# Last pass of a six-pass graph network on one core: rows closed in another order, four chunks' layers computed from split parts, steps spaced wider, adjacency splits queued 14 pieces ahead instead of 20

## The reference, cut to what matters

```python
# x: 4096 x 128, adj: 4096 x 4096, all float32
def gnn(x, adj, kernel, bias):                 # one product with adj, one layer
    return relu((adj @ x) @ kernel + bias)

def mlp(x, W1, b1, W2, b2, W3, b3):            # three 128 x 128 layers
    x = leaky_relu(x @ W1 + b1, 0.01)
    x = leaky_relu(x @ W2 + b2, 0.01)
    return leaky_relu(x @ W3 + b3, 0.01)

x = layernorm(x + gnn(x, adj, ...))
u = x
for _ in range(3):
    v = mlp(adj @ u, uv weights)
    u = mlp(adj @ v, vu weights)               # the third u is never used
x = layernorm(x + v)
```

## Time and profile before

| | us |
|---|---|
| median of 3 runs | 1168.94 |
| lowest and highest | 1168.66, 1168.98 |
| the profiled execution, its own time | 1168.49 |
| its span in the profile | 1166.7 |
| PE busy | 1153.5 (99% of the span) |
| DVE busy | 736.7 (63%) |
| ACT busy | 659.3 (57%) |

### The profile page before, as it was taken

The page is one execution under the profiler, slowest core; times in us unless marked ns, Lnnn a source line. Parts: engine busy times, 40 slices in busy tenths (PEclk is TensorE's granted clock), DMA queues, the critical chain, the costliest instruction groups (busy, mean ns, idle before and its releaser), DMA issues.

```text
span 1166.7 us, 13724 instructions
## 1 busy us (share of the span) xinstructions
PE 1153.5 (99%) x5242; PEld 954.0 (82%) x5242; DVE 736.7 (63%) x888; ACT 659.3 (57%) x811; POOL 4.9 (0%) x10
## 2 busy tenths in 40 slices
PE   7999999999999999999999999999999999999998
PEld 6888888888888888888888888888888888887876
DVE  7997676458555555555545746553566554678985
ACT  7765555346554555555444755553556544667874
POOL 0000000000000000000000000000000000000001
PEclk9999999999999999999999999999999999999999
DMA  9988786568356646555656636655575656579971
GB/s 383 405 301 322 251 270 198 200 216 288 120 205 217 210 157 213 199 195 181 205 188 220 238 124 211 205 179 198 192 242 165 212 186 230 166 292 356 312 281 36
DMA packets 72353, 261.60 MB, mean 224 GB/s; under 512 B 8032, under 2 KB 8800, under 8 KB 71264
## 3 DMA queue, kind: packets, MB, share of 16 engines
q1 hardware_dynamic: 72144, 260.61, 64.0%
q10 hardware_dynamic: 144, 0.13, 0.0%
HBM read 258.61 MB, written 2.10 MB: 223 GB/s over the span
## 4 chain that ended last, share of the span: by engine, by line
PE 94%; DMA 3%; DVE 1%; ACT 0%; SPq 0%; issue 0%; ACTq 0%
PE agg_ps L932 29%; PE agg_ps L925 28%; PE agg_ps L918 28%; PE pre_ps L829 4%; DMA adj_raw<-in_adj 3%; PE hid_ps L790 1%; PE hid_ps L792 1%; PE hid_ps L791 1%; DVE adj_lo L770 1%; PE hid_ps L851 1%; PE hid_ps L865 0%; ACT adj_hi L635 0%; DVE stats L648 0%; PE hid_ps L868 0%; SPq L496 0%
## 5 line engine op out<-in xcount | busy, mean ns | idle before, releaser
L770 DVE TENSOR_TENSOR adj_lo<-adj_raw,adj_hi 128x1024 fp32r<-128x1024 f32 x464 | 547.8, 1219 | 224.9 <-ACT adj_hi L635 219.6
L918 PE MATMUL agg_ps<-adj_hi,feat_hi 128*128 128x512 f32 x1484 | 586.4, 395 | 7.5 <-ACT adj_hi L635 7.5
L925 PE MATMUL agg_ps<-adj_hi,feat_lo 128*128 128x512 f32 x1484 | 579.3, 390 | 0.0
L635 ACT ACTIVATE adj_hi<-adj_raw 128x1024 fp32r<-128x1024 f32 x464 | 467.6, 1051 | 83.3 <-PE agg_ps L932 69.1
L932 PE MATMUL agg_ps<-adj_lo,feat_hi 128*128 128x512 f32 x1484 | 458.8, 390 | 0.2 <-DVE adj_lo L770 0.2
L918 PEld LDWEIGHTS agg_ps<-adj_hi,feat_hi 128*128 128x128 f32 x1484 | 279.6, 188 | 66.0 <-issue 9.4
L925 PEld LDWEIGHTS agg_ps<-adj_hi,feat_lo 128*128 128x128 f32 x1484 | 279.5, 188 | 59.1 <-issue 1.9
L932 PEld LDWEIGHTS agg_ps<-adj_lo,feat_hi 128*128 128x128 f32 x1484 | 278.9, 188 | 59.5 <-DVE adj_lo L770 1.1
L528 ACT ACTIVATE hid<-hid_ps,params 128x512 f32<-128x512 f32 (+2 forms) x82 | 55.1, 672 | 59.6 <-PE hid_ps L792 50.7
L600 ACT ACTIVATE in_hi<-part 128x512 fp32r<-128x512 f32 x24 | 15.2, 634 | 110.3 <-DVE part L759 110.3
L528 ACT ACTIVATE post<-pre 128x512 f32<-128x512 f32 x39 | 24.7, 632 | 88.0 <-DVE pre L737 88.0
(11 more groups left out here) (80 smaller groups left out, 389.8 us busy)
## 6 DMA issues: line engine op xcount, KB each, us to landing
adj_raw<-in_adj SPq DMA_DIRECT2D x472, 512.0 KB, 5.6
adj_raw<-in_adj SPq DMA_DIRECT2D x8, 1024.0 KB, 8.1
resid<-in_x SPq DMA_DIRECT2D x8, 256.0 KB, 8.1
out<-resid SPq DMA_DIRECT2D x7, 256.0 KB, 5.3
params<-in_weights SPq DMA_DIRECT2D x1, 386.0 KB, 5.1
b_row<-in_bias_rows SPq DMA_DIRECT2D x1, 128.0 KB, 5.7
out<-resid SPq DMA_DIRECT2D x2, 64.0 KB, 1.8
out<-resid ACTq DMA_DIRECT2D x1, 128.0 KB, 1.9
```

The lines of the kernel that those rows point to most:

```text
L635: act.activation(split_hi(b)[:, i * CHUNK:(i + pieces) * CHUNK], adj_raw[:, h % RAW, 0:pieces * CHUNK], ACT.Copy).then_inc(adj_hi_ready, 1)
L770: dve.tensor_tensor(split_lo(b)[:, slot], adj_raw[:, h % RAW, 0:pieces * CHUNK], split_hi(b)[:, slot].bitcast(F32), ALU.subtract).then_inc ...
L918: pe.matmul(group_bank(g), feat_hi[feats][:, tile(src, i)], split_hi(b)[:, piece(i)], start=start, stop=False)
L925: pe.matmul(group_bank(g), feat_lo[feats][:, tile(src, i)], split_hi(b)[:, piece(i)], start=False, stop=False)
```

## The change

The rows of the last pass are closed in the order 6, 1, 5, 4, 3, 2 (before: 6, 5, 4, 3, 1, 2). The first four chunks of the last pass (rows 0, 7, 6 and 1) are computed in parts, with a table of their own, LAST_PARTS. The LATE3 table goes, and LATE2 and LATE get wider distances. LAST_LEAD goes from 20 to 14.

```diff
-LEAD, FIRST_LEAD, LAST_LEAD, FIRST_ROWS = 12, 4, 20, 3
+LEAD, FIRST_LEAD, LAST_LEAD, FIRST_ROWS = 12, 4, 14, 3
...
+    LAST_PARTS: dict(dve_sum=0, act_in=3, dve_in=4, pe_hid1=10, act_hid1=11, dve_hid=13, pe_hid2=20, act_hid2=21,
+                     pe_out=25, dve_pre=25, act_post=28, dve_stats=29, act_std=32, dve_shift=33, act_norm=36),
     LAST: dict(dve_sum=0, act_in=0, pe_hid1=6, act_hid1=7, pe_hid2=10, act_hid2=11, pe_out=14, dve_pre=14,
                act_post=16, dve_stats=16, act_std=20, dve_shift=20, act_norm=24),
-    LATE3: dict(dve_sum=0, act_in=0, pe_hid1=6, act_hid1=7, pe_hid2=10, act_hid2=11, pe_out=14, dve_pre=14,
-                act_post=16, dve_stats=17, act_std=20, dve_shift=20, act_norm=24),
-    LATE2: dict(dve_sum=0, act_in=1, pe_hid1=4, act_hid1=5, pe_hid2=7, act_hid2=8, pe_out=9, dve_pre=10,
-                act_post=10, dve_stats=12, act_std=14, dve_shift=15, act_norm=16),
-    LATE: dict(dve_sum=0, act_in=1, pe_hid1=1, act_hid1=2, pe_hid2=3, act_hid2=5, pe_out=5, dve_pre=7, act_post=7,
-               dve_front=8, dve_total=8, dve_stats=9, act_std=12, dve_root=13, pool_norm=13),
+    LATE2: dict(dve_sum=0, act_in=0, pe_hid1=5, act_hid1=6, pe_hid2=9, act_hid2=10, pe_out=13, dve_pre=13,
+                act_post=14, dve_stats=15, act_std=18, dve_shift=18, act_norm=22),
+    LATE: dict(dve_sum=0, act_in=1, pe_hid1=3, act_hid1=4, pe_hid2=5, act_hid2=7, pe_out=7, dve_pre=9, act_post=9,
+               dve_front=10, dve_total=10, dve_stats=11, act_std=14, dve_root=15, pool_norm=15),
...
-LAST_ROWS = (6, 5, 4, 3, 1, 2)
+LAST_IN_PARTS = 4
+LAST_ROWS = (6, 1, 5, 4, 3, 2)
...
             return END2 if after < 0 else END if after == 0 else LATE if after == 1 else LATE2 if after == 2 \
-                else LATE3 if after == 3 else LAST
+                else LAST_PARTS if u < self.rows * (PASSES - 1) + LAST_IN_PARTS else LAST
...
-        return self.steps_of(u) in (IN_PARTS, TURN)
+        return self.steps_of(u) in (IN_PARTS, TURN, LAST_PARTS)
...
-                u = at(t, "dve_hid", HIDDEN)
+                u = at(t, "dve_hid", DEEP)
...
-                u = at(t, "dve_in", HIDDEN)
+                u = at(t, "dve_in", DEEP)
```

More of the change, by code:

```diff
@@ L40 @@
 HOLD = 3
-LEAD, FIRST_LEAD, LAST_LEAD, FIRST_ROWS = 12, 4, 20, 3
+LEAD, FIRST_LEAD, LAST_LEAD, FIRST_ROWS = 12, 4, 14, 3
 LOAD_GCN, LOAD_PARAMS = 24, 90
 W_SPLIT = 320
-IN_PARTS, TURN, LATE3, LATE2, LATE, END, END2 = "in_parts", "turn", "late3", "late2", "late", "end", "end2"
+IN_PARTS, TURN, LAST_PARTS, LATE2, LATE, END, END2 = "in_parts", "turn", "last_parts", "late2", "late", "end", "end2"
 STEPS = {
```

## The result

| | before | changed |
|---|---|---|
| median of 6 runs, us | 1168.72 | 1174.73 |
| lowest and highest | 1168.45, 1168.98 | 1174.15, 1174.85 |
| profiled execution | 1168.49 | 1174.76 |
| its span | 1166.7 | 1173.0 |

What follows compares the result with a forecast made beforehand. PE, busy 99% of the span, was taken to bound the kernel, with DVE near its limit. Waits of 7.8, less 0.3 waited before and 1.5 saved, gave +6.0: 1174.5 profiled, 1175.0 median, range 1172.5 to 1177 (62%).

Steps and rivals of the forecast that it cites:

- Part 1: PE's own work: eight float32 layers computed in parts save 0.185 us each, 1.5 us less.
- Part 2: Added work on DVE and ACT in the last pass makes PE wait at late steps, 7.8 us in all.
- first place: Second layer of row 6: DVE's `hid_lo` starts at 1103.0, so PE waits 1.6 us.
- all rounds: DVE's waits for ACT in the three stretches laid out: 1.8, 2.3 and 2.8 us.
- Second place: Second layer of row 5: ACT's hidden layer is late, PE waits 2.6 us, and 0.8 at the third layer.
- Third place: First layer of row 4: DVE's sum starts at 1140.4, so PE waits 1.8 us.
- The clock: Rival, 3%: waits of 2.6 us twice lower PE's granted clock, +3 us more, 1178.
- Part 3: What costs nothing: splits stay ahead of their use, wider tables fit; the lead alone is worth 0.3 us.
- The end: From the last row's cuts on, same operations in the same order: costed at nothing.
- DVE keeps up: Rival, 10%: DVE's 51.8 us of work fit PE's 53.3, PE keeps its 1.5 us gain: 1167.4.
- Half of it: Rival, 15%: only the first and third place are late, 3.5 us of waits, +1.7: 1170.6.
- Feed each other: Rival, 10%: late steps delay the next rows, another wait of 2 to 3 us at row 3 or final cuts: 1178.

Runs made afterwards that it cites:

- four_moved: Changed kernel with dve_hid 12 instead of 13, act_post 29 instead of 28, act_norm 39 instead of 36, lead 16 instead of 14, same work: 1167.23 us.
- five_placed: Changed kernel with a fifth chunk (row 5) in parts, five numbers of LAST_PARTS moved and lead 20: 1166.37 us.
- busy_pe: Changed kernel with nine added, never-read products on PE ahead of its wait for row 5's second layer: 1174.56 us.
- parts_only: Kernel before with rows 0, 7, 6 and 5 in parts by LAST_PARTS and row 4 by LAST; row order, LATE2, LATE and lead unchanged: 1171.85 us.
- lead20: Changed kernel with LAST_LEAD 20 again instead of 14: 1174.51 us.
- no_parts: Changed kernel with no chunk of the last pass in parts; row order, wider tables and lead of 14 kept: 1168.96 us.
- norm38: Changed kernel with act_norm of LAST_PARTS 38 instead of 36, so ACT's scaling stands two ticks later: 1170.48 us.
- norm34: Changed kernel with act_norm of LAST_PARTS 34 instead of 36, so ACT's scaling stands two ticks earlier: 1182.82 us.

## Why the prediction was right, and where not

The forecast was 1175.0, the measurement 1174.73. By its own steps, the excess at each place taken from distances between L933 rows, as above:

| step of the prediction | forecast | measured |
|---|---|---|
| second layer of row 6, waits for `hid_lo` | 1.6 | 1.7 |
| the small waits before row 5 | 0.4 + 0.2 | 0.3 + 0.2 |
| second layer of row 5, waits for ACT | 2.6 | 2.3 |
| slow clock behind it (a rival's, 3%) | 0 | 1.7 |
| third layer of row 5 | 0.8 | 0 |
| first layer of row 4, waits for `part` | 1.8 | 1.0 |
| first layer of row 3 | 0.4 | 0.6 |
| sum | 7.8 | 7.8 |
| waited before; layers in parts (both as in part 1) | -0.3 - 1.5 | -0.3 - 1.5 |

This makes +6.0, as forecast. The profiled execution became 6.27 us longer; what is more lies within the 0.37 by which it is behind already when row 0 closes. 0.33 of that are there at 300 us, where both kernels do the same, so it has nothing to do with the change.

The sum is right and its parts are not. PE's waits add up to 6.1 us and not 7.8 (the prediction expected 7 to 8 in the profile; the view of waits, which counts from modelled ends, has 4.6), and 1.7 us of slow matmuls stand in for the rest. That the total came out even so is in part luck, and in part the reason given under the clock.

**Part 1** is right: four_moved, where PE waits for almost nothing, is 1.4 us faster than before, and five_placed, with two layers more in parts, 2.4; 1.5 and 1.85 were to come from the layers and 0.3 from the wait that there was before, less the 0.5 left over in four_moved. That gives 1.3 and 2.15.

**Part 2, first place.** `hid_lo` was to start at 1103.0 and started at 1103.33; row 0 closed 0.37 us later than in the trace of before (ACT's copy starts at 1062.05 instead of 1061.68), and taken from there the step is exact. The step on which it rested, DVE's four waits for ACT, 1.8 in all, measured 0.52 + 0.34 + 0.24 + 0.29 = 1.4 in brackets. Each also costs the 0.09 us by which DVE's operations otherwise overlap (a split is 1.22 long and the next starts after 1.13), which makes 1.75. Over all rounds I had laid out 1.8 + 2.3 + 2.8 = 6.9. The view has 6.8, but that holds a wait of 1.24 that ended at 1079.99, ahead of the rounds; the other eleven are 5.6, or 6.6 with 0.09 for each. Where they come from I had laid out wrongly in part: ACT was to stand at the root each time, and of the four only the last (0.29) follows from that. The first stands behind `post`, which waited 1.74 us for DVE's bias, and the next two behind the scaling, which waited for `shift`. All the same they are ACT waiting for DVE and DVE then for ACT, and the experiments that moved steps to other ticks made them smaller and larger, and PE's waits with them. That is the shown cause: the places in the lists, with the same operations in them.

**Second place.** The chain was as laid out (scaling, split, `post`, split, hidden layer): the last was to start at 1126.0 and did at 1126.19. The wait was 2.3 instead of 2.6, since PE asked at 1124.6 instead of 1124.1.

**Third place.** Here the working has a slip: 1126.7 + 10.2 + 1.8 + 0.8 is 1139.5 and not 1139.3, so by its own terms the wait is 1.6. With the clock kept up (busy_pe) it is 1.6.

**The clock** is where I was wrong. I gave it 3%, priced at +3 us, since the clock in the earlier trace rows stayed at 1.00 through 7.5 us without matmuls in the first 30. That was a misreading, as PE's own rows behind those 7.5 us show in the kernel before:

```profile
8.53 0.63 PE L918 MATMUL agg_ps<-adj_hi,feat_hi 128*128 128x512 f32 x1
8.96 0.63 PE L925 MATMUL agg_ps<-adj_hi,feat_lo 128*128 128x512 f32 x1
```

They follow each other at 0.43 us, as the slow ones above, and so do all from 8.1 to 13.2 us, where the column of the clock says 1.00. So the first stretch spoke for slow matmuls behind idle time and not against them; why the column doesn't show them there, no run tells. The rival's mechanism occurred: 0.50 for some 3.4 us behind the second place. Its price was wrong the other way: busy_pe puts it at nothing that can be told. What the table shows as 0 and 1.0 at the next two places, where 0.8 and 1.8 were forecast, is the same 1.7 us seen from the other side: with the clock kept up the distances between the rows give 0.8 and 1.6 there. The sum came out right since what was late there was not PE but DVE and ACT, and their times were right: `part` of row 4 was to start at 1140.4 and started at 1140.56.
The Trainium skill ("TensorE: Matmul & The Clock Gate", section Why this matters for your kernels) warns against longer idle gaps between bursts of matmuls, because the clock then falls to half. The trace has such a fall, to 0.50, behind a standstill of 2.3 us; parts_only has a standstill as long without one.

**Part 3.** The lead was laid out at 0.3; lead20 gives 0.2, which can't be told from nothing. The end, costed at nothing, is within no_parts' 1168.96, so it costs nothing by itself.

**The rivals.** "DVE keeps up" (10%, 1167.4) did not come, but four_moved is this rival made true by four numbers, at 1167.23. "Half of it" did not come either, since all three places were late; nearest in time is norm38 (1170.48), with smaller waits at all three. "Feed each other" did not come, and norm34 (1182.82) looks like it: a wait of 1.5 us is followed by others of 4.1 and 3.3. That a few ticks in one table hold 1167.2 and 1182.8 says that the layout in order was needed; the balance of DVE's 51.8 us of work against PE's 53.3 gave no sign of 6 us.

## What to carry to other kernels

Where two engines work through fixed lists and hand work to each other, the busy time of neither tells whether a third one will wait: lay out both lists in order with the durations of the trace, and look for a step that the third needs soon standing behind one that waits for the other. When such a step turns up, first try it at other places among its neighbours, together with them, before taking its work away; here that made +6.0 us into -1.4 with the same operations. And price a slow clock only after asking what the engine would have waited for next: time that would have been waited anyway is not lost.

## What was not expected of the hardware

The granted clock fell to 0.50 with some standstills of PE and not with others of the same length. It fell with the one of 2.13 us in the changed kernel (and the same in lead20, clock 0.94 from 1110 to 1140) and with the ones of 4.05 and 3.3 us in norm34; it did not with 2.28 us in parts_only. In the changed kernel it fell 0.9 us after PE had gone on (at 1127.8), in norm34 already inside the standstill of 4.05 us (1104.1 to 1108.1; the stretch from 1106 to 1107 shows 0.64 and the next 0.50). PE at the standstill in parts_only, and the stretches around it:

```profile
1125.09 0.47 PE L791 MATMUL hid_ps<-hid_hi,w_hi 128*128 128x512 f32 x1 [2.28 <-DVE hid_lo L746]
```

```profile
1122.00:1125.00 3.00, 0.80 (x4) 0.34 (x2) 1.89 (x3) 3.00 (x5) 0.00 (x0) 1.00 0.83 294
1125.00:1128.00 3.00, 2.91 (x13) 2.44 (x14) 3.00 (x3) 3.00 (x4) 0.00 (x0) 1.00 0.64 203
1128.00:1131.00 3.00, 3.00 (x19) 2.63 (x18) 3.00 (x4) 2.29 (x3) 0.00 (x0) 1.00 0.91 221
```

The changed kernel and parts_only differ in what follows the gap (a float32 layer there, a layer in parts here) and in where in the run the gap lies. What follows can't be needed for a fall, since in norm34 it came before PE had gone on. What decides between gaps of about 2.2 us stays open; no run was made to tell that.
